# A factorised-interaction recommender tower on one core: five chunks instead of four, doubles turned in pairs

## The reference

```python
pij = jnp.einsum('bpe,dpe,bpd->bp', e[:, rows], kernel, e[:, cols])
z = pij @ W.T + b                                   # (2048, 256)
h = jnp.concatenate([z, dense_ctx], axis=1)         # (2048, 272)
h = jnp.maximum(h @ W_top1 + b_top1, 0.0)           # 512
h = jnp.maximum(h @ W_top2 + b_top2, 0.0)           # 256
y = h @ W_top3
```

## Time and profile before

| | us |
|---|---|
| median of 3 runs (1359.11 to 1363.39) | 1359.52 |
| profiled execution | 1367.28 |
| its span | 1365.4 |
| TensorE busy, 11888 matmul instructions | 1075.3 |
| VectorE busy | 615.0 |
| ScalarE busy | 560.2 |
| GpSimd busy (512 gathers) | 483.7 |
| mean granted clock | 0.831 |

### The profile page before, as it was taken

One profiled execution on the slowest core, in us unless ns is written; L12 is line 12 of the kernel. 1 busy time (PEld: TensorE's weight loads), 2 busy tenths in 40 slices (PEclk: granted clock), 3 DMA queues, 4 the chain that ended last, 5 costly groups with the idle time before them and its releaser, 6 DMA issues.

```text
span 1365.4 us, 29877 instructions
## 1 busy us (share of the span) xinstructions
PE 1075.3 (79%) x11888; PEld 350.7 (26%) x11888; DVE 615.0 (45%) x559; ACT 560.2 (41%) x4205; POOL 483.7 (35%) x517
## 2 busy tenths in 40 slices
PE   4110335779999977879999985968899999999997
PEld 2000001122334311222323320222222333333333
DVE  2000001143656622234437951334334997668990
ACT  0000000084655601024447960024425993669961
POOL 6777771544232264544442035444434000000000
PEclk9555555688998866679999995779889999999999
DMA  8111110100000010100000001000000000000000
GB/s 322 26 26 27 26 26 5 20 18 17 11 14 11 10 22 15 19 17 17 17 17 10 3 13 20 16 18 18 17 14 17 3 3 3 2 2 2 3 3 2
DMA packets 21570, 29.10 MB, mean 21 GB/s; under 512 B 11108, under 2 KB 11620, under 8 KB 20920
## 3 DMA queue, kind: packets, MB, share of 16 engines
q0 software_dynamic: 16384, 16.81, 6.3%
q1 hardware_dynamic: 3368, 8.79, 1.7%
q10 hardware_dynamic: 1680, 1.61, 0.3%
HBM read 27.17 MB, written 0.01 MB: 20 GB/s over the span
## 4 chain that ended last, share of the span: by engine, by line
PE 68%; another core or an unknown queue 14%; issue 12%; DVE 3%; ACT 2%; DMA 1%; SPq 0%; ACTq 0%; DVEq 0%
PE bilinear L580 36%; PE sums L622 16%; PE bilinear L594 8%; PE bilinear L648 6%; PE bilinear L557 2%; ACT batch_prod L444 1%; DVE prod L499 1%; DVE batch_prod L510 1%; DVE w_comb_sb L480 0%; DVE prod L494 0%; DMA b_sb<-b_top 0%; DVE prod L496 0%; PE sums L606 0%; PE bilinear L530 0%
## 5 line engine op out<-in xcount | busy, mean ns | idle before, releaser
L580 PE MATMUL bilinear<-emb_t,k_sb 64*32 64x512 f32 x6144 | 623.0, 636 | 208.9 <-issue 197.3
L499 DVE TENSOR_TENSOR prod<-bilinear,emb_t 128x1024 f32<-128x1024 f32 x352 | 419.2, 1218 | 499.3 <-remote 375.7
L444 ACT ACTIVATE batch_prod<-batch_prod 128x64 f32<-128x64 f32 x2048 | 490.1, 242 | 103.6 <-DVE batch_prod L510 98.5
L365 POOL DMA_INDIRECT emb<-table,ids_sb x384 | 362.3, 944 | 440.5 <-PE bilinear L557 329.9
L444 ACT ACTIVATION_READ_ACCUMULATOR batch_prod<-batch_prod 128x1 f32 x2048 | 386.3, 189 | 1.4 <-issue 1.3
L622 PE MATMUL sums<-prod,row_sel 64*32 64x512 f32 x2944 | 293.1, 634 | 35.0 <-issue 21.4
L580 PEld LDWEIGHTS bilinear<-emb_t,k_sb 64*32 64x32 f32 x6144 | 158.8, 111 | 575.5 <-issue 516.6
L403 ACT ACTIVATE emb_t<-bilinear 128x512 f32<-128x512 f32 x64 | 37.9, 593 | 480.5 <-PE bilinear L557 285.1
L510 DVE TENSOR_TENSOR batch_prod<-bilinear,emb_first 128x1024 f32<-128x1024 f32 x128 | 156.0, 1218 | 143.6 <-remote 112.6
L594 PE MATMUL bilinear<-k_sb,emb_t 64*32 64x512 f32 x2048 | 172.8, 622 | 2.2 <-issue 0.9
L365 POOL DMA_INDIRECT emb_first<-table,ids_sb x128 | 120.9, 945 | 126.6 <-DVE batch_prod L510 83.4
(11 more groups left out here) (25 smaller groups left out, 117.7 us busy)
## 6 DMA issues: line engine op xcount, KB each, us to landing
emb<-table,ids_sb POOLq DMA_INDIRECT x384
k_sb<-k_slots SPq DMA_DIRECT2D x2, 1088.0 KB
emb_first<-table,ids_sb POOLq DMA_INDIRECT x128
k_sb<-k_slots SPq DMA_DIRECT2D x1, 1600.0 KB
k_sb<-k_slots SPq DMA_DIRECT2D x1, 1472.0 KB
k_sb<-k_slots SPq DMA_DIRECT2D x1, 960.0 KB
k_sb<-k_slots SPq DMA_DIRECT2D x1, 896.0 KB
k_sb<-k_slots SPq DMA_DIRECT2D x1, 576.0 KB
```

The source lines that it names most:

```text
L365: nc.gpsimd.indirect_dma_start(fields_of(i, j, t)[:, f % 2, :], None, tables[f], bass.IndirectOffsetOnAxis(ap=ids_sb[:, start + t, f:f + 1 ...
L444: last = nc.scalar.activation(products, products, ACT.Copy, accum_out=batch_sums[:, t, half, row + f:row + f + 1])
L499: last = nc.vector.tensor_tensor(prod[:, at:at + 2, 0:n], bilinear[:, bank:bank + 2, 0:n], emb_t[:, j:j + 1, 0:n].to_broadcast([P, 2, n]), ...
L580: last = nc.tensor.matmul(bilinear[col:col + QUARTER, bank + row // EMB, 0:n], k_sb[row:row + EMB, operand, col:col + QUARTER], emb_t[row: ...
```

## The change

Five chunks of 2, 4, 4, 4 and 2 tiles. From chunk 1 on a turn takes two doubles: eight transposes (four in chunk 4) into both banks of one ring place and one copy by ScalarE; they stand behind slots 85, 89 and 93 of the chunk before and 2, 10, 18, 26 and 34 of their own. Layers start behind slot 12. A small chunk has 16 batches. Reduces go one at a time, not ahead of a unit behind which ScalarE has another step. The dense features are loaded untransposed, one transfer a chunk, into free columns of `batch_sums` before the join, which turns them with the sums; the pair rows are numbered anew so that one block of 16 rows stays free, and the fold is copied in four pieces instead of ten.

```diff
-CHUNK_TILES = (4, 4, 4, 4)
+CHUNK_TILES = (2, 4, 4, 4, 2)
...
-FIRST_LAYER = 10
+FIRST_LAYER = 12
 LAYER_EVERY = 4
 REDUCE_LAG = 2
-TURNS_EARLY = {83: 0, 85: 1, 87: 2, 89: 3, 91: 4, 93: 5}
-TURNS = {1: 6, 4: 7, 8: 8, 12: 9, 16: 10, 20: 11, 24: 12, 28: 13, 32: 14, 36: 15}
+TURNS_EARLY = {85: 0, 89: 2, 93: 4}
+TURNS = {2: 6, 10: 8, 18: 10, 26: 12, 34: 14}
 BATCH_FROM, BATCH_EVERY = 4, 2.5
-FIRST_BATCH_FROM, FIRST_BATCHES, THEN_FROM, THEN_EVERY = 8, 8, 16, 2.8
+FIRST_BATCH_FROM, FIRST_BATCHES, THEN_FROM, THEN_EVERY = 8, 4, 16, 5.6
 BATCHED_AT = NQUADS - (NGROUPS - 1) * GROUP_QUADS
-BATCHED_ROWS = BATCHED // (HALVES * 4)
-SPARE_AT = BATCHED_AT + BATCHED_ROWS
-SPARE = 32 - SPARE_AT
+DENSE_AT = P - DENSE
+BATCHED_ROWS = [(half, 32 * b + pos) for half in range(HALVES) for b in range(4) for pos in range(BATCHED_AT, 32)][:BATCHED]
...
-        after = [BATCH_FROM + n * BATCH_EVERY for n in range(len(batches))]
+        after = [BATCH_FROM + n * BATCH_EVERY * 4 / tiles for n in range(len(batches))]
...
 def program():
+    behind = [[] for _ in range(len(ALL_UNITS) + SUM_LAG + 2)]
+    for at, (kind, i, which) in enumerate(ALL_UNITS):
+        if kind != "slot":
+            continue
+        if i > 0 and which in TURNS:
+            behind[at].append(("turn", i, (TURNS[which], 2)))
+        if i + 1 < NCHUNKS and which in TURNS_EARLY:
+            behind[at].append(("turn", i + 1, (TURNS_EARLY[which], 2)))
+        k = (which - FIRST_LAYER) // LAYER_EVERY
+        if i > 0 and (which - FIRST_LAYER) % LAYER_EVERY == 0 and 0 <= k < NOUTS:
+            behind[at].append(("layer", i - 1, k))
+        behind[at + SUM_LAG] += [("sum", i, q) for q in range(NQUADS) if last_slot_of_quad(q) == which]
+        if which == NSLOTS - 1:
+            behind[at + SUM_LAG + 1].append(("join", i, 0))
+
+    def for_scalar(at):
+
+        return any(kind in ("turn", "layer", "join") or (kind == "sum" and (which + 1) % GROUP_QUADS == 0)
+                   for kind, i, which in behind[at])
+
     steps = [("fold", 0, 0)]
     turned = 0
-    sums, reduces = [], []
+    reduces = []
     for at, (kind, i, which) in enumerate(ALL_UNITS):
         if i == 0:
             needed = max(row_of(unit) for unit in ALL_UNITS[at:at + TURNED_BEFORE] if unit[1] == 0)
-            steps += [("turn", 0, j) for j in range(turned, needed + 1)]
+            steps += [("turn", 0, (j, 1)) for j in range(turned, needed + 1)]
             turned = max(turned, needed + 1)
         steps.append((kind, i, which))
...
-        while reduces and reduces[0][0] <= at:
+        if kind == "batch":
+            reduces += [(at + REDUCE_LAG, ("reduce", i, (*which, half))) for half in range(HALVES)]
+        steps += behind[at]
+
+        if reduces and reduces[0][0] <= at and not for_scalar(at + 1):
             steps.append(reduces.pop(0)[1])
-        while sums and sums[0][0] <= at:
-            steps.append(sums.pop(0)[1])
-    steps += [step for at, step in reduces] + [step for at, step in sums]
+    steps += [step for _, step in reduces]
+    for late in behind[len(ALL_UNITS):]:
+        steps += late
     steps += [("layer", NCHUNKS - 1, k) for k in range(NOUTS)]
     return steps
...
+TURN_OF = {(i, j + n): use for (i, (j, several)), use in TURN_USE.items() for n in range(several)}
...
+        def store(sp, i):
+            at = CHUNKS[i][0] * P
+            sp.wait_ge(s_layer_out, (i + 1) * NOUTS)
+            sp.dma_start(out[:, at:at + cols(i)], y_sb[:, 0:cols(i)]).then_inc(s_stored, 16)
...
-                sp.wait_ge(s_sums_out, (i + 1) * NSUMS)
-                for b in range(8):
-                    row = 32 * (b % 4) + SPARE_AT
-                    sp.dma_start(sums_sb[row:row + SPARE, NSUMS - HALVES + b // 4, 0:cols(i)],
...
+            sp.wait_ge(s_consts, 4)
+            for i, (start, tiles) in enumerate(CHUNKS):
+                wait(sp, s_joined, i)
+                sp.dma_start(batch_sums[:, 0:tiles, HALVES - 1, DENSE_AT:],
+                             dense[start * P:(start + tiles) * P, :].rearrange("(t p) f -> p t f", p=P)).then_inc(s_dense, 16)
+                if i > 0:
+                    store(sp, i - 1)
+            store(sp, NCHUNKS - 1)
...
-                        pool.wait_ge(s_turned, TURN_USE[i - 1, j] + 1)
+                        pool.wait_ge(s_turned, TURN_OF[i - 1, j] + 1)
                     elif i > 1:
 
-                        pool.wait_ge(s_turned, TURN_USE[i - 2, j] + 1)
+                        pool.wait_ge(s_turned, TURN_OF[i - 2, j] + 1)
                         pool.wait_ge(s_batch_prod, BATCHES_TO[i - 1])
...
-            def turn_out(i, j):
-                act.wait_ge(s_turned, TURN_USE[i, j] + 1)
+            def turn_out(i, j, several):
+                act.wait_ge(s_turned, TURN_USE[i, (j, several)] + 1)
                 if i > 0:
 
-                    act.wait_ge(s_prod, (i - 1) * NSLOTS + LAST_SLOT[j] + 1)
-                    if j in BATCHED_ROWS_OF:
-                        act.wait_ge(s_batch_prod, BATCH_USE[i - 1, (j, CHUNKS[i - 1][1] - 1)] + 1)
-                nc.scalar.activation(emb_t[:, j, 0:cols(i)], bilinear[:, ring_bank("turn", i, j), 0:cols(i)],
+                    doubles = range(j, j + several)
+                    act.wait_ge(s_prod, (i - 1) * NSLOTS + max(LAST_SLOT[d] for d in doubles) + 1)
+                    batched = [d for d in doubles if d in BATCHED_ROWS_OF]
+                    if batched:
+                        act.wait_ge(s_batch_prod, BATCH_USE[i - 1, (batched[-1], CHUNKS[i - 1][1] - 1)] + 1)
+                bank, n = ring_bank("turn", i, (j, several)), cols(i)
+                nc.scalar.activation(emb_t[:, j:j + several, 0:n], bilinear[:, bank:bank + several, 0:n],
                                      ACT.Copy).then_inc(s_emb_t, 1)
...
-                if g >= NSUMS - HALVES:
-                    parts_out = [slice(32 * b, 32 * b + SPARE_AT) for b in range(4)]
-                else:
-                    parts_out = [slice(0, P)]
-                for rows in parts_out:
-                    last = nc.vector.tensor_copy(w_comb_sb[rows, g, :], bilinear[rows, g, :])
-                last.then_inc(s_folded_out, 1)
+                rows = slice(0, P if g < NSUMS - 1 else DENSE_AT)
+                nc.vector.tensor_copy(w_comb_sb[rows, g, :], bilinear[rows, g, :]).then_inc(s_folded_out, 1)
...
-            def turn(i, j):
-                ring_free("turn", i, j)
-                pe.wait_ge(*gathered(i, j))
-                for t in range(CHUNKS[i][1]):
-                    last = nc.tensor.transpose(bilinear[:, ring_bank("turn", i, j), t * P:(t + 1) * P],
-                                               fields_of(i, j, t), ident[:])
+            def turn(i, j, several):
+                ring_free("turn", i, (j, several))
+                bank = ring_bank("turn", i, (j, several))
+                for n in range(several):
+                    pe.wait_ge(*gathered(i, j + n))
+                    for t in range(CHUNKS[i][1]):
+                        last = nc.tensor.transpose(bilinear[:, bank + n, t * P:(t + 1) * P], fields_of(i, j + n, t),
+                                                   ident[:])
                 last.then_inc(s_turned, 1)
...
+                pe.wait_ge(s_dense, 16 * (i + 1))
...
-                        if term == NSUMS - HALVES:
-                            pe.wait_ge(s_dense, (i + 1) * (16 * 8))
```

More of the change, by code:

```diff
@@ L124, in block_pairs, with batched_row @@
     return (2 * j, 2 * m + half), (2 * j + 1, 2 * m + half)
-def batched_row(m, c):
-    half, n = divmod(((m - BATCHED_ROWS_OF[0]) * 2 + c) * BATCHED_FIELDS, 4 * BATCHED_ROWS)
-    return half, n // BATCHED_ROWS * 32 + BATCHED_AT + n % BATCHED_ROWS
+def batched_row(m, c, f):
+    return BATCHED_ROWS[((m - BATCHED_ROWS_OF[0]) * 2 + c) * BATCHED_FIELDS + f]
 def sum_rows():
@@ L140, in sum_rows @@
         for c in range(2):
-            half, row = batched_row(m, c)
-            for r in range(BATCHED_FIELDS):
-                rows[(NSUMS - HALVES + half) * P + row + r] = pair_index(r, 2 * m + c)
+            for f in range(BATCHED_FIELDS):
+                half, row = batched_row(m, c, f)
+                rows[(NSUMS - HALVES + half) * P + row] = pair_index(f, 2 * m + c)
     return rows
@@ L188, in program @@
             needed = max(row_of(unit) for unit in ALL_UNITS[at:at + TURNED_BEFORE] if unit[1] == 0)
-            steps += [("turn", 0, j) for j in range(turned, needed + 1)]
+            steps += [("turn", 0, (j, 1)) for j in range(turned, needed + 1)]
             turned = max(turned, needed + 1)
         steps.append((kind, i, which))
[L192 to L203, removed]
-        else:
-            reduces += [(at + REDUCE_LAG * (half + 1), ("reduce", i, (*which, half))) for half in range(HALVES)]
-        while reduces and reduces[0][0] <= at:
+        if kind == "batch":
+            reduces += [(at + REDUCE_LAG, ("reduce", i, (*which, half))) for half in range(HALVES)]
+        steps += behind[at]
```

(37 more changed lines are left out.)

10 lines of the change are left out of this document (2 added, 8 removed).

## The result

The changed kernel takes 1409.22 us (median of 4, 1401.14 to 1413.14) against 1359.32 us (1357.87 to 1363.39): ratio 1.0354, interval 1.03 to 1.0409, slower. The forecast was 1389, with a range of 1365 to 1415. Both kernels were timed where bursts of gathers nearly stop the other engines, which the prediction calls the hold. The experiments found chips where there is no hold: there the changed kernel takes 852.1 us and the kernel before 851.3, ratio 1.0013 (1.0003 to 1.0022). So the forecast is right for a chip with the hold, and it did not know that there are others; on one of those it would have been off by more than 500 us.

The account below looks back on a forecast made before the run. Matmul work (740 us) and 512 gathers (1.22 us each) stand one after the other, nearly without overlap. Terms -4 + 14 + 11 + 16 + 2 - 4 - 5 = +30 on the 1359.5 us median give 1389, range 1365 to 1415.

Parts of the forecast that it names:

- The sum: Whole kernel: all terms together +30 us, put on the median of 1359.5 us.
- Term 1: Start: first gather burst ends 80 us sooner, but the 64 gathers moved later pay it back; -4 us.
- term 2: Layers in chunks 1 to 3: pair turns leave fewer layers hidden in the hold, 31 us against 45; +14 us.
- the first rival: Start not paid back: the 64 moved gathers cost 0.80 us each instead of 1.20; 1345 us, chance 0.20.
- Terms 3 and 4: Chunk 0: half-width matmuls pass the hold with less work, +11 us; narrow chunks 0 and 4 cost extra, +16 us.
- Term 4: Chunks 0 and 4: at half width VectorE becomes the bound, 8 us for each chunk; +16 us.
- Term 6: Visits: turns go from 64 to 48, layers 28 to 35, joins 4 to 5, at 0.5 us each; -4 us.
- Term 7: End of the last chunk: latency of dense transfers, evictions and last multiplies goes; -5 us.
- The clock rival: Chunks 1 and 2: bursts of 16 hold the granted clock low, +36 us on the sum; 1425 us, chance 0.15.
- The rule rival: Gathers never hold compute engines, so the start's 80 us stay saved, -80 + 16; 1296 us, chance 0.03.

Follow-up runs that it names:

- Experiment 4: Without the hold: four full chunks, single turns, only dense path and reduce order changed, 851.2 us; kernel after with chunks 4, 4, 4, 2, 2, 858.52 us.
- experiment 5: With the hold, kernel before 1390.85 us: its layers moved behind slots 40 to 64, 1426.62 us; kernel after with four full chunks, pair turns, 1401.14 us.

## Why the prediction was right, step by step

- **The sum.** +30 was forecast. The profiled executions differ by 39 us (spans 1365.4 and 1404.6). The medians differ by 50, as the profiled run of before lay 8 us above its median and that of after 3 below. Elapsed time less 740 us of work is 625 us before and 665 after: by the forecast's prices the matmul work is the same, and all 39 us are in the loss. The number came out 20 us low, inside the range. That it came out at all hangs on the chip: nothing in the prediction asks whether the hold is there on every one.
- **Term 1, start.** Right. GpSimd's first burst ended at 124.7 us, TensorE came back at 139, and the first 96 gathers cost (143.6 - 4.5 - 18) / 96 = 1.26 each, 121 us. The 16 later ones cost 20 us. Chunk 3's 48, at the 0.97 of its first 40, cost 47, where the forecast had 45 (57.6 less the 12.5 that layers save in term 2). Together that is 188 us for what cost 205 before, -17 as forecast (-4 and -12.5), so nearly all of the 80 us were paid back. This rules out the first rival, which wanted 0.80 for those gathers.
- **Terms 3 and 4, narrow chunk 0.** Right in size: 88 gathers at 1.45 instead of 1.25 are +18, the long burst of 40 behind them +3, and the forecast had +19 for both there. The third row above agrees with the mechanism: what passes the hold is a few instructions (24, against 34 and 36 in the earlier trace rows), each with half the work. How the 18 us divide between the terms is not shown.
- **Term 4, narrow chunk 4.** Right. VectorE's 512-element op took 685 ns. Of the windows, which lie behind the last layers of chunk 4, the first is from the kernel after with the hold, the second from it without:

```profile
L510 DVE TENSOR_TENSOR prod<-bilinear,emb_t 128x512 f32<-128x512 f32 x176 | 114.0, 685 | 277.7 <-remote 243.8 <-PE bilinear L593 33.6
```

```profile
1336.00:1379.00 43.00, 41.67 (x1304) 23.10 (x1298) 40.23 (x59) 38.86 (x314) 0.00 (x0) 1.00 0.02 4
```

```profile
782.50:825.00 42.50, 41.17 (x1293) 22.73 (x1279) 39.92 (x59) 38.36 (x311) 0.00 (x0) 1.00 0.02 4
```

  1304 matmuls are 49 slots with their share, 0.88 us each, and 1293 are 48, 0.89 each, where the forecast had 0.85 to 0.9. VectorE is busy for 94% of either window, while TensorE's work is 38 us in each. Experiment 4 agrees: two narrow chunks at the end cost 16 us. The forecast's 1.42 for VectorE at full width is a slip, as it counts half of the batches: in 1240 to 1320 us VectorE is busy 78.59 us for 50 slots, 1.57 each, against TensorE's 1.6. So at full width the two are nearly level, and only at half width does VectorE fall behind.
- **Term 2, layers in the hold.** The mechanism is shown: layers moved out of the hold cost 36 us (experiment 5). The size was short. The gathers in chunks 1 and 2 of the kernel after cost 230 us, where the forecast's prices give 216. Layers 0, 2 and 4 saved 1.4 us in chunk 1 and 6.4 in chunk 2, where I took all of their work, 5.3 and 10.5. The first two bursts of 16 of a chunk cost 1.33 per gather, not 1.27. These 14 us are more than the 9 between +30 and +39, so the other terms together were some 5 too high.
- **Term 6, visits.** Right for the turns, as far as chips without the hold show it. 16 visits fewer at 0.5 us are 8 us, of which the term took back 4 for more layers and joins; pair turns gave 9 us with four chunks and 6 with five. Elapsed less work of a chunk falls from 8.9 to 5.5 us.
- **Term 7, end.** Too large, -2 instead of -5: elapsed less work of the end, from the last join on, went from 31.8 - 24.8 = 7.0 us to 17.0 - 12.3 = 4.7. With the dense path alone (experiment 4) the end takes 30.2 us instead of 31.8.
- **The clock rival** did not come in its size. The granted clock did fall, from 0.96 and 0.91 to 0.80 and 0.81 in the rows with bursts of 16. But the gathers in chunks 1 and 2 cost 14 us more than the forecast's prices, where the rival wanted 36. How much of these 14 is the clock's is not shown.
- **The rule rival.** The Trainium skill's sentence (SBUF — State Buffer, "Who interferes with whom") says that a DMA never contends with a compute engine. It fits chips 0, 3 and 6, where TensorE goes on beside the gathers (2036 matmuls in 154 us on chip 6), and neither the chip of the first timing nor chip 14. The price for it, 1296, was wrong as well. It took the hold away only from the 80 us at the start; without the hold both kernels are at 852, TensorE is busy for 93% of the span of before, and its waits for gathers are as long in both kernels.

What stays open is what the hold is. It follows GpSimd's gathers by microseconds, lets a few instructions through, and was there in the first timing and on one later chip of four. The transfers themselves are not slower in it. In the kernel before, the 16384 packets of the gathers' queue take 6.3% of 16 x 1365.4 us with the hold and 10.2% of 16 x 849.8 us without, 84 and 85 ns each. Whether plain transfers hold too was tried only where nothing holds, and no kernel with the gathers issued otherwise ran with the hold.

## What to carry to other kernels

- Run the kernel before again beside every experiment, and compare it with its first time. Here a factor of 1.6 lay between two chips, and a tuning choice (turns in pairs) was worth -1.1% on one and +0.75% on the other.
- Where something lets only so many instructions through, put those with the most work in each there, and don't split work into narrower ones.
- Time that is cut at the start is a gain only if what was moved finds cover where it lands. Price it there.
- Read an engine's share in a window that holds one kind of work; a few layers in it hide which engine sets the pace.

## What the runs showed of the hardware

- One program, the kernel before, takes 1359 us in the first timing, 1391 on chip 14 and 851 to 852 on chips 0, 3 and 6, each steady within 0.7%. With the hold a long burst of gathers leaves TensorE 56 matmuls in 154 us, without it 2036.
- The hold lasts 1.40 us for each gather of a long burst, though GpSimd starts one every 1.25: matmuls flow again at 139.1 us after the burst of 96 that starts at 4.5 (kernel after), and at 229.2 us after the burst of 160 that starts at 5.7 (kernel before). So it outlasts the last gather's issue by 14 and 24 us.
- GpSimd starts an indirect gather of 128 rows every 1.25 us with the hold and without. It starts a plain transfer of the same size every 0.53 us, and the sync engine starts one every 0.47 us (both without the hold).
